# Linear attention in a fused two-layer block: how gate, adding of experts, divides and norms are spread over the engines

## The reference

```
mu = mean(x); var = mean((x - mu)**2)
xn = (x - mu) * rsqrt(var + LN_EPS) * ln_g + ln_b
q, k, v = split(xn @ w_qkv + b_qkv, 3)
gate = sigmoid(xn @ w_gate + b_gate)
k = k * gate
q = elu(q) + 1 ;  k = elu(k) + 1
attn = einsum('btd,bsd->bts', q, k) * mask        # causal
out_num = einsum('bts,bsd->btd', attn, v)
out_den = sum(q * cumsum(k), -1) + DEN_EPS
return out_num / out_den @ w_proj + b_proj
```

## Time and profile before

| | |
|---|---|
| time, three runs | 1312.21 us median (1311.05 to 1316.88) |
| profiled execution | 1309.46 us, of it the span 1307.6 us |
| mean granted TensorE clock | 0.96 of full |
| busy: TensorE, VectorE, ScalarE, GpSimd | 1154.7, 917.1, 850.9, 790.0 us |
| this stage | from 1080.87 us, first add, to the last transposes at 1148.38 us |
| before it and after it | experts of the first mixture up to 1078.4 us; router of the second from 1152.75 us |

### The profile page before, as it was taken

One profiled execution on the slowest core, in us unless ns is written; L12 is line 12 of the kernel. 1 busy time (PEld: TensorE's weight loads), 2 busy tenths in 40 slices (PEclk: granted clock), 3 DMA queues, 4 the chain that ended last, 5 costly groups with the idle time before them and its releaser, 6 DMA issues.

```text
span 1307.6 us, 36404 instructions
## 1 busy us (share of the span) xinstructions
PE 1154.7 (88%) x12703; PEld 865.8 (66%) x12704; DVE 917.1 (70%) x2475; ACT 850.9 (65%) x2476; POOL 790.0 (60%) x705
## 2 busy tenths in 40 slices
PE   5899898999888999969998989999979994888996
PEld 2577685776765666636766857767669882648985
DVE  6898668898775666668886688877754337775334
ACT  3899857999643555559998589995435553334554
POOL 6788438887456453258883487763377753237773
PEclk8899999999988999989999999999879997988998
DMA  7001100011000000000111000113147752025775
GB/s 224 17 22 27 35 11 20 21 26 27 22 11 3 3 3 3 3 1 18 26 26 28 16 12 22 26 26 93 33 129 219 207 148 57 1 81 153 226 203 162
DMA packets 69808, 78.21 MB, mean 60 GB/s; under 512 B 25094, under 2 KB 50501, under 8 KB 69509
## 3 DMA queue, kind: packets, MB, share of 16 engines
q1 hardware_dynamic: 64133, 64.70, 17.7%
q0 software_dynamic: 5504, 11.28, 3.6%
HBM read 54.60 MB, written 8.78 MB: 48 GB/s over the span
## 4 chain that ended last, share of the span: by engine, by line
PE 28%; DVE 7%; DMA 6%; ACT 5%; POOL 4%; issue 3%; SPq 1%; POOLq 0%; ACTq 0%; DVEq 0%
PE bank L1846 5%; DMA y_rows<-stg,inv_u 3%; PE bank L916 3%; ACT pB L795 3%; PE bank L1860 2%; DMA arena<-arena 2%; POOL arena L2176 2%; POOL y_rows L2182 2%; PE bank L637 2%; PE bank L928 1%; PE bank L600 1%; PE bank L545 1%; PE bank L559 1%; PE bank L551 1%; PE bank L612 1%
## 5 line engine op out<-in xcount | busy, mean ns | idle before, releaser
L864 POOL TENSOR_TENSOR rn<-ss,mhalf 128x16 f32<-128x16 f32 x64 | 187.6, 2932 | 6.8
L2104 DVE SCALAR_TENSOR_TENSOR act_b<-bank,vec,gl 128x128 f32<-128x128 f32 x258 | 74.9, 345 | 131.4 <-ACT gl L1927 113.3
L1846 PE MATMUL bank<-arena 128*128 128x128 f32 x1032 | 135.0, 282 | 1.3 <-issue 1.3
L1846 PEld LDWEIGHTS bank<-arena 128*128 128x128 f32 x1032 | 125.5, 196 | 5.6 <-issue 4.5
L795 ACT ACTIVATE pA<-bank,nb,rn 128x128 f32<-128x128 f32 x256 | 113.5, 485 | 2.5 <-DVE nb L726 2.5
L795 ACT ACTIVATE pB<-bank,nb,rn 128x128 f32<-128x128 f32 x256 | 113.3, 478 | 1.7 <-DVE nb L726 1.7
L850 POOL TENSOR_TENSOR arena<-arena 128x512 f32<-128x512 f32 x64 | 81.6, 1275 | 48.3 <-DVE nb L726 37.1
L1927 ACT ACTIVATE gl<-bank,vec 128x128 f32<-128x128 f32 x258 | 76.0, 365 | 50.4 <-PE bank L1846 34.2
L1609 DVE TENSOR_REDUCE act_b<-bank 128x2 f32<-128x512 f32 x128 | 79.6, 685 | 39.7 <-PE bank L1491 39.7
L857 POOL TENSOR_TENSOR arena<-arena 128x512 f32<-128x512 f32 x64 | 81.3, 1271 | 43.0 <-DVE arena L689 16.3
L2182 POOL DMA_INDIRECT y_rows<-stg,inv_u x86 | 84.9, 988 | 34.0 <-issue 17.1
(11 more groups left out here) (334 smaller groups left out, 3141.6 us busy)
## 6 DMA issues: line engine op xcount, KB each, us to landing
arena<-in_L_ffn_We SPq DMA_DIRECT2D x86, 384.0 KB
arena<-arena SPq DMA_DIRECT2D x64, 128.0 KB, 2.3
arena<-in_L_ffn_We SPq DMA_DIRECT2D x3, 768.0 KB, 7.2
arena<-U SPq DMA_DIRECT2D x32, 64.0 KB
u_rows<-U SPq DMA_DIRECT2D x2, 1024.0 KB, 5.6
U<-y_rows SPq DMA_DIRECT2D x8, 256.0 KB, 4.2
uT<-y_rows SPq DMA_DIRECT2D x8, 256.0 KB, 5.0
arena<-U SPq DMA_DIRECT2D x32, 63.5 KB
```

Source lines behind the costliest of these rows:

```text
L864: pool.tensor_tensor(rn[:, q % 4, :, :], ss[:, 1, :].rearrange("p (a h) -> p a h", a=2), mhalf[:, :].rearrange("p (a h) -> p a h", a=2), A ...
L1846: m = pe.matmul(bank[q % 2][:, j * P:(j + 1) * P], we1[q][:, half * HR + j * P:half * HR + (j + 1) * P], xT[:, q, :], start=True, stop=True)
```

## The change

Five things change, all between the gather of the first mixture's results and the last transposes of the linear attention:

- The second expert's rows are multiplied by their weights on ScalarE (`scale_second`, four instructions a chunk), and VectorE adds four weighted tiles and then one 128x512 tensor. The final adding of the second mixture already worked so and keeps its instructions.
- The gate is Tanh of half the value, then times 0.5 plus 0.5 on GpSimd (`gates` in `la_pool`). Tanh and Exp are loaded with one table.
- There is no separate first part: `turned`, `gate_proj` and the adding of experts join the loop over chunks, two chunks ahead. The turned rows, the gate and v have one bank each, so `v_proj(c)` waits for the Tanh of c and `gate_proj(c)` for the copy of v of c-1.
- The division's multiply (`divided`) goes from VectorE to ScalarE, four instructions a chunk.
- The norm of the result (`x_normed`) goes from VectorE to ScalarE, four instructions a chunk with scale and bias; GpSimd makes the bias -mean x inverse root with two more instructions a chunk.

What stands in the queues now. ScalarE in the loop, before: from the Exp work of chunk 1 to that of chunk 2. `pB` is z, `gl` and `pA` are k, `act_b` and `arena` are v, `pT` is the turned output.

The core of the diff (line numbers of before at the left of each hunk's head):

```diff
@@ -2130 @@ adding of experts
-            for n in range(2):
-                for t in range(c * CT, (c + 1) * CT):
-                    if n:
-                        dve.wait_ge(s.x_sum, sums(k0, c) + t - c * CT + 1)
-                    dve.scalar_tensor_tensor(X[:, t, :], gathered(n, c)[:, t - c * CT, :], wc[:, n, t:t + 1], X[:, t, :],
-                                             ALU.mult, ALU.add).then_inc(s.x_sum, 1)
...
+        def scale_second(act, k0, c):
+            act.wait_ge((s.gat0, s.gat1, s.gat2, s.gat3)[c], 16 * 2 * (k0 + 1))
             for t in range(CT):
                 g = gathered(1, c)[:, t, :]
                 m = act.activation(g, g, ACT.Identity, scale=wc[:, 1, c * CT + t:c * CT + t + 1])
             m.then_inc(s.x_scaled, 1)
...
@@ -2245 @@ banks
-        LB_T, LB_G, LB_Q, LB_K, LB_V, LB_A, LB_N, LB_X = (B[4], B[5]), (B[2], B[3]), B[0], B[1], B[3], (B[4], B[5]), (B[6], B[7]), B[2]
+        LB_T, LB_G, LB_Q, LB_K, LB_V, LB_A, LB_N, LB_X = B[2], B[3], B[0], B[1], B[3], (B[4], B[5]), (B[6], B[7]), B[2]
...
@@ la_pe @@
             def gate_proj(c):
                 pe.wait_ge(s.uT_ready, LA_T + c + 1)
-                if c > 1:
-                    pe.wait_ge(s.n_gate, c - 1)
+                if c:
+                    pe.wait_ge(s.n_v, c)
...
             def v_proj(c):
-                if c:
-                    pe.wait_ge(s.n_v, c)
-                else:
-                    pe.wait_ge(s.n_gate, NCH)
+                pe.wait_ge(s.n_tanh, c + 1)
...
-            turned(0)
...
-            for i in range(-1, NCH + 3):
+            for i in range(-2, NCH + 3):
                 if has(i - 1):
                     out_proj(i - 1)
                 if has(i - 2):
                     x_turned(i - 2)
                 if has(i):
                     sums(i)
                 if has(i + 2):
+                    turned(i + 2)
+                if has(i + 1):
+                    v_proj(i + 1)
+                if has(i + 2):
+                    gate_proj(i + 2)
                     k_proj(i + 2)
                 if has(i + 1):
-                    if i >= 0:
-                        v_proj(i + 1)
                     scores(i + 1)
...
@@ la_act @@
-                act.activation(la_chunk(gate, c), LB_G[c % 2][:, :], ACT.Sigmoid, bias=vec[:, V_LGATE:V_LGATE + 1])\
-                    .then_inc(s.n_gate, 1)
+                act.activation(la_chunk(gate, c), LB_G[:, :], ACT.Tanh, bias=labias[:, 2:3], scale=0.5)\
+                    .then_inc(s.n_tanh, 1)
...
+            def x_normed(c):
+                act.wait_ge(s.rs_ready, LA_RS + NCH + c + 1)
+                for t in range(c * CT, (c + 1) * CT):
+                    m = act.activation(U[:, t, :], X[:, t, :], ACT.Identity, bias=nmr[:, 1, t:t + 1],
+                                       scale=rs[:, 1, t:t + 1])
+                m.then_inc(s.ln_done, 1)
+
+            def divided(c):
+                act.wait_ge(s.n_rec, c + 1)
+                if c:
+                    act.wait_ge(s.n_oT_ps, c)
+                for j in range(CT):
+                    o0 = (j % 2) * (D + 1)
+                    m = act.activation(osb[:, j, :], LB_N[j // 2][:, o0:o0 + D], ACT.Copy, scale=ndr[:, 1, j:j + 1])
+                m.then_inc(s.n_o, 1)
...
-            act.preload_act_table(ACT.Sigmoid)
...
+            act.preload_act_table(ACT.Exp)
+            for c in range(3):
+                scale_second(act, 0, c)
+            normed(0)
+            gates(0)
+            scale_second(act, 0, 3)
+            normed(1)
+            v_out(0)
+            exps(0)
+            gates(1)
+            for i in range(NCH + 2):
                 if has(i - 1):
                     o_out(i - 1)
                 if has(i + 1):
+                    v_out(i + 1)
                     exps(i + 1)
-                    v_out(i + 1)
                 if has(i - 2):
                     x_out(i - 2)
+                if has(i + 2):
+                    normed(i + 2)
+                if has(i):
+                    divided(i)
+                if has(i + 2):
+                    gates(i + 2)
+                if has(i - 1):
+                    x_normed(i - 1)
...
@@ la_dve @@
-                for j in range(CT):
-                    o0 = (j % 2) * (D + 1)
-                    m = dve.tensor_scalar(osb[:, j, :], LB_N[j // 2][:, o0:o0 + D], ndr[:, 1, j:j + 1], None, ALU.mult)
-                m.then_inc(s.n_o, 1)
...
             added(0)
-            for c in range(1, NCH):
-                added(c)
-                normed(c - 1, 0)
-            normed(NCH - 1, 0)
-            for i in range(-1, NCH + 1):
+            added(1)
+            normed(0)
+            added(2)
+            normed(1)
+            gated(0)
+            added(3)
+            features(0)
+            for i in range(NCH + 1):
                 if has(i + 1):
                     gated(i + 1)
                 if has(i):
                     masked(i)
+                if has(i + 2):
+                    normed(i + 2)
                 if has(i - 1):
                     result(i - 1)
                 if has(i + 1):
                     features(i + 1)
                 if has(i):
-                    divided(i)
-                if has(i - 1):
-                    normed(i - 1, 1)
+                    inverted(i)
...
@@ la_pool @@
+            def gates(c):
+                pool.wait_ge(s.n_tanh, c + 1)
+                pool.tensor_scalar(la_chunk(gate, c), la_chunk(gate, c), 0.5, 0.5, ALU.mult, ALU.add)\
+                    .then_inc(s.n_gate, 1)
...
+            for c in range(3):
                 power(c, 0)
+            gates(0)
+            x_bias(0)
             v_bias(0)
+            power(3, 0)
+            gates(1)
+            for i in range(NCH + 1):
+                if has(i - 1):
+                    power(i - 1, 1)
+                if has(i + 1):
+                    x_bias(i + 1)
+                    v_bias(i + 1)
+                if has(i + 2):
+                    gates(i + 2)
```

More of the change, by code:

```diff
@@ L2165, in add_last @@
                                          xc[:, t, :], ALU.mult, ALU.add).then_inc(s.x_sum, 1)
-            dve.wait_ge(s.x_scaled, c + 1)
-            dve.wait_ge(s.x_sum, sums(1, c) + CT)
+            dve.wait_ge(s.x_scaled, k0 * NCH + c + 1)
+            dve.wait_ge(s.x_sum, sums(k0, c) + CT)
             dve.tensor_tensor(xc, xc, gathered(1, c), ALU.add).then_inc(s.x_sum, 1)
@@ L2380, in normed @@
                 act.wait_ge(s.ln_ps, LA_T + c + 1)
-                act.activation(la_chunk(uT, c), LB_T[c % 2][:, :], ACT.Identity, bias=vec[:, V_LNB:V_LNB + 1],
+                act.activation(la_chunk(uT, c), LB_T[:, :], ACT.Identity, bias=vec[:, V_LNB:V_LNB + 1],
                                scale=vec[:, V_LNG:V_LNG + 1]).then_inc(s.uT_ready, 1)
@@ L2420, in has @@
                 return 0 <= c < NCH
-            act.preload_act_table(ACT.Sigmoid)
+            act.preload_act_table(ACT.Exp)
+            for c in range(3):
+                scale_second(act, 0, c)
             normed(0)
-            for c in range(1, NCH):
-                normed(c)
-                gates(c - 1)
-            gates(NCH - 1)
-            act.preload_act_table(ACT.Exp)
-            for i in range(-1, NCH + 2):
+            gates(0)
[5 more added lines that the diff above has]
+            for i in range(NCH + 2):
                 if has(i - 1):
@@ L2483, in masked, with inverted @@
                     dve.tensor_tensor(am[b][:, :], LB_A[b][:, 0:384], causal[:, :], ALU.mult).then_inc(s.n_am, 1)
-            def divided(c):
+            def inverted(c):
                 for b in range(2):
@@ L2544, in power @@
                 pool.wait_ge(s.stats_ready, LA_RS + k * NCH + c + 1)
-                pool.tensor_scalar(rs[:, 0, ts], mv[:, ts, 1], a_, b_, ALU.mult, ALU.add).then_inc(s.p_self, 1)
+                if not k:
+                    pool.tensor_scalar(rs[:, 0, ts], mv[:, ts, 1], a_, b_, ALU.mult, ALU.add).then_inc(s.p_self, 1)
+                    pool.wait_ge(s.p_self, next(p_own))
+                    pool.tensor_tensor(rs[:, 1, ts], rs[:, 0, ts], mhalf[:, 0:CT], ALU.pow).then_inc(s.rs_ready, 1)
+                    return
+                pool.tensor_scalar(rs[:, 0, ts], mv[:, ts, 1], a_, b_, ALU.mult, ALU.add)
+                pool.tensor_scalar(nmr[:, 0, ts], mv[:, ts, 0], -1.0, 0.0, ALU.mult, ALU.add).then_inc(s.p_self, 1)
                 pool.wait_ge(s.p_self, next(p_own))
-                pool.tensor_tensor(rs[:, 1, ts], rs[:, 0, ts], mhalf[:, 0:CT], ALU.pow).then_inc(s.rs_ready, 1)
+                pool.tensor_tensor(rs[:, 1, ts], rs[:, 0, ts], mhalf[:, 0:CT], ALU.pow).then_inc(s.p_self, 1)
+                pool.wait_ge(s.p_self, next(p_own))
+                pool.tensor_tensor(nmr[:, 1, ts], nmr[:, 0, ts], rs[:, 1, ts], ALU.mult).then_inc(s.rs_ready, 1)
             def x_bias(c):
@@ L2557, in v_bias, with has @@
```

(20 more changed lines are left out.)

55 lines of the change are left out of this document (19 added, 36 removed).

## The result

| | before | after |
|---|---|---|
| time, 11 runs each | 1310.40 us (1307.53 to 1316.88) | 1322.86 us (1317.83 to 1323.66) |
| profiled execution, span | 1309.46, 1307.6 us | 1322.87, 1321.0 us |
| first add to first `result` | 40.22 us | 37.28 us |
| the three periods of `result` | 8.68, 7.42, 6.60 us | 15.18, 13.26, 8.86 us |
| last `result` to last transposes | 4.59 us | 5.65 us |

The ratio is 1.0076, 95% interval 1.0059 to 1.0094: 10 us slower, some 8 to 12; the two medians are 12.5 us apart. In the two profiled executions the spans differ by 13.4 us: 12.7 in the stage (80.23 - 67.51), 1.3 behind it, and -0.6 ahead of it.

The account below looks back on a forecast made before the run. It took VectorE's result starts as the stage's beat in a well-filled loop, bounded after the change by a cycle of queues. Terms -6.1 + 4.98 + 6.2 + 1.1 + 3.0 = +9.2 us on 1312.21 gave 1321, range 1314 to 1329.

Parts of the forecast that it names:

- The mechanism: Loop queues: ScalarE waits to copy v ahead of Exp work, and TensorE's gate product waits for turned rows behind it.
- The loop, +4.98 and +6.2: Periods between results: the first 13.66 instead of 8.68 us, the last two together 20.2 instead of 14.02.
- The walk: Adding up instruction durations and waits along the engines' queues through entry and loop, giving periods 13.66, 12.75 and 7.45 us.
- The entry, -6.1: First add to first result: attention of chunk 0 starts before other chunks are added, so its result comes 6.1 us earlier.
- The gates at 1.04: GpSimd's 0.5x + 0.5 over 128x512 taken as 1.04 us, like a multiply of that size.
- The clock, +3.0: TensorE, idle in three long periods, then runs at a lower clock: +3.0 us, bounds 0 and 7.
- The rival of dear gates: GpSimd's gate form takes 3.76 us, giving +16, 1328; grouped with a long lower clock (+13, 1325), chance 0.17.
- Meetings of GpSimd and VectorE, 1.3: GpSimd's bias additions and VectorE instructions hold each other up: 1.3 us in all, bounds 0 and 5.
- The exit, +1.1: Last result to last transposes: extra GpSimd instructions and ScalarE's norm make 5.7 instead of 4.59 us; bounds 0.6 and 2.
- Division and norm off VectorE, counted as no gain: Loop: taking both off saves VectorE 2.2 us a chunk, but VectorE now waits, so nothing is counted.
- The clock holds: Rival: full clock throughout, gates at 0.52 us and half the port meetings, +5.0 us, 1317; chance 0.25.
- VectorE was the beat: Rival: loop periods follow VectorE's queue and fall by 2.2 us each, -11.6 in all, 1300.6 us; chance 0.05.

Follow-up runs that it names:

- e1: The changed kernel with ScalarE's two Relus and two Exps of the next chunk ahead of its copy of v; ratio 0.9997 to before, stage 68.88 us.
- e7: The changed kernel plus 13 unused 128-column products on TensorE behind each chunk's v projection in the loop; ratio 1.0062 to before, stage 74.20 us.
- e3: The changed kernel with the division's multiply and the last norm back on VectorE; ratio 1.0051 to before, stage 74.50 us.
- e5: Two-part order and banks of before, with the change's Tanh gate, GpSimd half step and second-expert weighting, division and last norm on VectorE; ratio 0.9964, stage 63.97 us.
- e6: The changed kernel with exponentials ahead of the copy of v, and division and last norm back on VectorE; ratio 0.9977 to before, stage 63.13 us.
- e8: The changed kernel itself, unaltered, run and profiled again; ratio 1.0103 to before, stage 78.25 us.

## Why the prediction was right, step by step

**The mechanism was right.** ScalarE stands before the copies of v, TensorE before the gate's product; e1 shortens the second wait from 3.49 to 1.35 us with one line. The sign and the range came out; the loss was +9.2 by forecast, +12.7 and +10.7 in the stages of two profiles and about +10 by the ratio. That 1321 lies so close to 1322.86 is partly luck: it was built on the median of three runs, 1312.21, which stands 1.8 above that of eleven, and for the profiled execution the forecast, 1318.7, was 4.2 short. With e7 as the changed kernel at full clock in the loop, the steps can be compared one by one:

- *The loop, +4.98 and +6.2.* The walk gave periods of 13.66, 12.75 and 7.45; e7 has 13.73, 12.35 and 7.40. These terms were +5.05 and +5.73. The agreement of the last two is weaker than it looks: the steps told for 12.75 add up to 13.1 (13.66 - 3.9 + 0.9 + 1.0 + 1.4), and 7.45 stands there without working.
- *The entry, -6.1.* In e7 it is -5.15 (35.07 against 40.22). In after it is -2.94, since the lower level from 1108 to 1114 falls into it; the walk had the later half of the entry at full clock and left this to the clock's term.
- *The gates at 1.04.* GpSimd took 0.62:

```profile
1111.00 0.62 POOL L2571 TENSOR_SCALAR arena<-arena 128x512 f32<-128x512 f32 x1 [4.49 <-ACT arena L2364]
```

  The rival of dear gates, 3.76, is out. The fill of 0.52 in the earlier trace rows was the better neighbour. The 769 ns of the GPSIMD Engine Reference, section "Performance versus the Vector engine" of the Trainium skill, were nearer than my value, and still high for this form.
- *Meetings of GpSimd and VectorE, 1.3.* The k feature took 0.69, 0.87 and 1.28 us in the three periods. The longest, with what ran beside it:

```profile
1136.63 1.27 POOL L2562 TENSOR_TENSOR X<-X,lbp_row 128x512 f32<-128x512 f32 x1
...
1137.85 1.18 POOL L2567 TENSOR_TENSOR act_b<-act_b,lbv_row 128x512 f32<-128x512 f32 x1
...
1138.29 1.28 DVE L2477 SCALAR_TENSOR_TENSOR gl<-gl,pB 128x512 f32<-128x512 f32 x1 [3.53 <-ACT pB L2376]
```

  That is 0.8 us beyond three lone ones, a little under my 1.3.
- *The exit, +1.1.* 5.65 against 4.59, +1.06, with ScalarE's norm at 1.65 (I had about 1.6). In e3, e5 and e6, where VectorE does it, the exit is 4.59 or 4.60.
- *The clock, +3.0.* This is the term that was mis-sized: 6.0 and 4.1 us in the two profiles. The bounds were 0 and 7, and the middle was chosen. One cause of the size is a misread row. The "60% more" comes from the 3.25 us of two gate products in the kernel before, but the first of them began at full clock:

```profile
1102.50:1103.00 0.50, 0.50 (x4) 0.26 (x2) 0.17 (x1) 0.24 (x1) 0.50 (x1) 0.94 0.00 0
1103.00:1106.00 3.00, 2.81 (x4) 0.62 (x2) 0.00 (x0) 1.38 (x3) 0.36 (x1) 0.50 0.00 0
```

  Wholly at the lower level a burst takes nearly twice as long: from the gate product at 1108.12 to the q product behind the scores after took 6.04 us, and e7 3.13. With that the upper bound would have been about 11 instead of 7, an estimate from 3.9 us a burst. The other cause is that in after the clock fell a fourth time, in the last period and on into the exit, which the term did not have; e8 has two falls before its exit. Two stretches of after:

```profile
1141.00:1147.00 6.00, 5.22 (x23) 4.33 (x23) 2.08 (x5) 2.98 (x9) 0.00 (x0) 0.53 0.00 0
1151.00:1160.00 9.00, 5.95 (x32) 5.74 (x29) 1.94 (x9) 3.41 (x10) 1.59 (x4) 0.53 0.00 1
```

  With the clock taken as after less e7, -5.15 + 5.05 + 5.73 + 1.06 + 6.03 = 12.7, the stage's difference.
- *Division and norm off VectorE, counted as no gain.* Right as far as VectorE goes. As a cost on ScalarE they were in the walk for the copy (1.4) and the exit; that is 2.5, and e7 against e3 gives 3.05 at full clock. e1 against e6 (68.88 and 63.13) gives 5.75, but e1 has stretches at the lower level in its loop and e6 has none, so part of it is clock.

**The rivals.** "The clock holds" is out, since the clock did not hold; at full clock e7 measured +6.7, where this rival had +5.0 and the forecast without its clock term +6.2. "VectorE was the beat" is out: VectorE is busy for 6.35 of 16 us. Tanh brought no table loads into the loop.

## What to carry to other kernels

- When stages are joined into one pipeline, walk each queue with the question "what is already ready behind this waiting instruction?". Here one copy that waited for TensorE stood ahead of four instructions whose inputs were there, and cost 11 us of a stage of 80; the joined pipeline with a written-out order, and with division and last norm back on VectorE, gained 11 us on the kernel before.
- Work moved to the less busy engine is only free if nothing urgent stands behind it in that engine's queue. ScalarE was busy for 35% of the loop before and the 2.8 us a chunk put on it still cost 3.05 us of the stage at full clock.
- Price the lower clock in full, from rows that lie wholly at one level, for every burst of TensorE that the change puts behind a long wait, in the entry too. It can also take a gain back in some executions: profile twice before a gain of 3 us in one profile is believed.

## What the runs showed of the hardware

- The granted clock is not fixed by the program. In one execution of the changed kernel both gate products in question took 2.07 us, in the other one took 2.00 and one 1.13 (rows of e8 above), each time behind the same wait of 3.49 us.
- 13 unused products in each of three waits of TensorE saved 4.1 us of the stage (78.25 to 74.20, one profile each), and 5.4 us by the medians of that batch (1322.05 and 1316.62).
- GpSimd's multiply-and-add of one 128x512 tensor takes 0.62 us, its addition of two 1.18 to 1.28.
